# Group statistics with a PSUM operand and half a batch earlier, and GpSimd adding seven of eight key tiles

## The chip, the cores and the metric

One Trainium2 chip, one of its cores. The metric is the device time of one execution in microseconds (us), the median of several runs. The engines are TensorE (PE), VectorE (DVE), ScalarE (ACT), GpSimd (POOL) and SyncE (SP, which only starts DMAs here). [...] SBUF is the large on-chip memory.

## What is computed

The input x has 8 batches of 256 channels by 32 x 32 positions, float32. Four blocks follow each other:

```python
x = L0(x)   # attention over 1024 positions in 32 latent channels, then over 128 concepts, both added to x
x = L1(x)   # 10 class maps per position, normalised, a gate per class from their mean, added to x
x = L2(x)   # group norm (32 groups of 8 channels), qkv, attention with 8 heads of 32 channels
            #   over 1024 positions, projection, added to x
x = L3(x)   # group norm, qkv, attention between the 8 heads at each position, projection, added to x
```

L2 is the longest. Its core, for each batch and head, is

```python
weight = softmax(einsum('bct,bcs->bts', q * scale, k * scale))
a = einsum('bts,bcs->bct', weight, v)
```

and before it, as before L3, stands the group norm: the mean and variance of 8 channels by 1024 positions, by which x is shifted and scaled.

## The kernel before, in words

All of a batch's 256 channels lie on 128 partitions in two parts (t = 0, 1). The attention of L0 and L2 runs in **windows**. A window handles four heads at once, so L0 has two windows (four batches each) and L2 has sixteen, two for each batch: `par` 0 with the first four heads and `par` 1 with the others. A window has 16 steps, 8 key tiles (`mt`) of 128 keys for each of two halves of 512 queries. In a step TensorE makes the scores of one key tile for four heads (`scores`, L604, four matmuls for each head), ScalarE takes their exponentials into `PR` (L995), and TensorE multiplies the exponentials of the step before with v into the bank `AV` (`values`, L630). `PR` holds four steps.

The softmax needs a maximum for each query ahead of the scores. Maxima of the coming half are made as further jobs: one `max` job is four matmuls (L592) and four row maxima on VectorE (L1249). Scores, maxima and all small products share a ring of seven PSUM banks; each engine walks the same written order of uses (`Ring`), and TensorE waits when the bank's last reader isn't done.

**The sums of the softmax.** The sum over keys of the exponentials is made for each half. GpSimd adds the exponentials of tiles 0 to 5 (`POOL_TILES`) into `ACC`: five additions for each of two head pairs, ten instructions at L1158. Then TensorE, in the job `sums` (L646), in the first step of the next half, sums over partitions with a matrix of ones: tiles 6 and 7 straight from `PR` (L652) and `ACC` (L657), for four heads each. GpSimd's first addition of a half waits until the sums of the half before have read `ACC` (`half_done`). ScalarE copies the sums and `AV` away (`keep_half`, L962), a DMA folds the sums into `R16`, VectorE takes the reciprocal in step 2 (`invert`, L1266), a DMA returns it in step 3 (`return_inverse`), and in step 5 TensorE spreads it and VectorE multiplies (`spread`, `normalise`).

**The order of the jobs** is written by `window_jobs` (L110): for each step a list, in which every engine finds its part. Eight `max` jobs lie in the first seven steps of a half, two of them in the first. Query and key products (`qk`), v products (`v`) of the coming window and the output products of the batch before (`post`) are spread over the steps.

**The group statistics** of the next batch stand in the second half of the `par` 0 window (in the last batch: of the last window, for L3). `statistics` (L1278) reads the batch from `XIN` in SBUF with four `bn_stats` and two `bn_aggr` in step 8. `group_sums(0)` (L682) in step 10 averages the channel means over a group on TensorE; `group_stats(0)` (L1289) copies the mean (`MG`), subtracts (`DEV`, L1294), squares (L1295) and adds the variance (`S2`, L1296). Step 12 has the second group sum; then GpSimd makes the scale and shift (`norm_factors`, L1121) and writes the normalised batch `XN` (L1138). SyncE loads the next batch into `XIN` once that is done (`sp_iteration`, L469).

L3 has no windows: for each of 64 token tiles GpSimd multiplies 7 of 8 heads' weights with v (L1184), VectorE the eighth (L1589), VectorE sums (L1600), and TensorE projects. `statistics` and `group_stats` of coming batches stand in VectorE's order there too (L1626, L1636).

Of the kernel before, what the change touches and what calls it, by code (L numbers as in the profile page):

```python
# [25 lines left out]
D = 32  # L26
# [6 lines left out]
POOL_TILES = (0, 1, 2, 3, 4, 5)  # L33
POOL_SUMS = len(POOL_TILES) - 1
INVERT_AT = 2
RETURN_AT = 3
SPREAD_AT = 5
# [72 lines left out]
def window_jobs(post=False, nxt=True, gn=False, trail=True, single=False):  # L110
# [45 lines left out]
def after_jobs():  # L156
# [3 lines left out]
    jobs[2].append(("spread", -1))  # L160
# [21 lines left out]
def program(nc, x, w_l0, w_o, concepts, concepts_t, gammas, conv_w, conv_wt, conv_b, lin1_t, lin2_t,  # L182
# [8 lines left out]
    with ctx:  # L191
# [208 lines left out]
        def iteration(i, window):  # L400
# [144 lines left out]
        def _(pe):  # L545
# [84 lines left out]
            def values(u, par, s):  # L630
                half, mt = s // MT, s % MT
                if mt == 0:

                    wait(pe, half_kept, 2 * (2 * u + half))
# [69 lines left out]
            def window(u, par, jobs, i):  # L704
                for s in range(STEPS):
# [3 lines left out]
                    elif ("sums",) in jobs[0]:  # L709
                        values(u - 1, 1 - par, STEPS - 1)  # L710
                    for job in jobs[s]:
# [20 lines left out]
                        elif job[0] == "gn":  # L732
                            group_sums(job[1], i + 1)
# [224 lines left out]
        def _(act):  # L958
# [3 lines left out]
            def keep_half(u, par, half):  # L962

                wait(act, half_done, 2 * u + half + 1)
                wait(act, norm_done, 2 * u + half)
                nc.scalar.activation(RC[:, :], RING[ring.place()], ACT.Copy).then_inc(half_kept, 1)
                nc.scalar.activation(OH[par][half], AV[:, :], ACT.Copy).then_inc(half_kept, 1)

                wait(act, half_kept, 2 * (2 * u + half) + 1)
# [9 lines left out]
            def window(u, par, jobs, i):  # L979
                early = par == 1 and i is None  # L980
                for s in range(STEPS):
                    for h in range(H):
# [3 lines left out]
                        if one == 0:  # L986
# [6 lines left out]
                            else:  # L993
# [4 lines left out]
                                             ).then_inc(exp_done, 1)  # L998
                    for job in jobs[s]:
                        if job[0] == "sums" and s == 0:  # L1000
                            keep_half(u - 1, 1 - par, 1)
                        elif job[0] == "sums":
                            keep_half(u, par, 0)
                        else:
                            ring.skip(places(job, i is None))
                    if s == (1 if early else RETURN_AT) and ("sums",) in jobs[0]:
# [34 lines left out]
            keep_half(1, 1, 1)  # L1041
# [46 lines left out]
            keep_half(2 * B + 1, 1, 1)  # L1088
# [29 lines left out]
        def _(pool):  # L1118
# [22 lines left out]
            def window(u, par, jobs, i):  # L1141
                for s in range(STEPS):
# [17 lines left out]
                    if jobs and ("gn", 1) in jobs[s]:  # L1160
                        if par == 0:
# [39 lines left out]
        def _(dve):  # L1201
# [76 lines left out]
            def statistics(batch):  # L1278
                wait(dve, xin_in, 16 * (batch + 1))
                src = XIN if not isinstance(batch, int) or batch <= B else xn3(batch - B)  # L1280
                for t in range(CT):
# [3 lines left out]
                link(nc.vector.bn_aggr(MV[:, 0, :], BN6[:, 0]))  # L1285
                link(nc.vector.bn_aggr(MV[:, 1, :], BN6[:, 1]))
                dve.sem_inc(gn_ready, 1)
# [426 lines left out]
```

## Time and profile before

| | us |
|---|---|
| median of 3 runs | 2064.46 (2063.97 to 2068.48) |
| the profiled execution | 2065.67 |
| its span, first to last instruction | 2063.7 |
| L0 and L1, up to the first window of L2 | 0 to 452 |
| L2, sixteen windows | 452 to 1614 |
| L3 | 1614 to 2064 |

The profile is of one execution. Its page gives the busy time of each engine and the costliest groups of instructions; the timeline gives instructions in order of time, neighbours of one kind merged ("x4" is four of them), and in square brackets the idle time of the engine before and what ended it. A matmul of float32 is two passes in the trace, so a group of four column-tiled matmuls is "x8".

### The profile page before, as it was taken

Reading aid. Unit: us, or ns where it says so; the run is one execution under the profiler, and the core shown is the slowest. Engines: PE = TensorE matmul, PEld = TensorE weight load, DVE = VectorE, ACT = ScalarE, POOL = GpSimd, SP = SyncE. Lnnn points to the kernel's source line nnn. Section 1 sums busy time; section 2 is a strip of 40 time slices with the busy share of each in tenths; the row PEclk is TensorE's granted clock in tenths of the full one; section 3 lists DMA queues with packets and bytes.
Section 4 is the critical chain, followed back from the end, with each engine's and each line's share of the span. In section 5 each row is a group of like instructions: output and inputs, shape, how many; then the busy total and the mean of one; then the engine's idle time right before and its main releaser. Section 6 shows DMA issues by size and latency. Waiting matters only on the chain.

```text
span 2063.7 us, 37560 instructions
## 1 busy us (share of the span) xinstructions
PE 1820.6 (88%) x15416; PEld 811.3 (39%) x15416; DVE 1485.6 (72%) x2203; ACT 786.5 (38%) x1546; POOL 1189.5 (58%) x509
## 2 busy tenths in 40 slices
PE   5987876879999999999999999999999868888884
PEld 2332322334444433433443443434443444554541
DVE  5666657787776777777777777787776148888875
ACT  0441220014454554553544544544545323333320
POOL 0471210016586675756756666567676238888896
PEclk8898888879999999999999999999999989999996
DMA  5000011030000101001001001001001121222121
GB/s 175 1 2 0 1 48 73 0 123 27 22 2 5 59 1 43 22 2 62 2 2 63 2 2 63 2 1 62 2 2 42 42 68 28 87 74 84 48 70 43
DMA packets 48160, 75.10 MB, mean 36 GB/s; under 512 B 30532, under 2 KB 30838, under 8 KB 47990
## 3 DMA queue, kind: packets, MB, share of 16 engines
q1 hardware_dynamic: 38486, 72.11, 9.9%
q8 instruction: 122, 2.00, 0.4%
q10 hardware_dynamic: 9504, 0.59, 0.3%
q14 instruction: 48, 0.39, 0.1%
HBM read 44.83 MB, written 25.17 MB: 34 GB/s over the span
## 4 chain that ended last, share of the span: by engine, by line
PE 72%; DVE 18%; issue 3%; ACT 3%; DMA 2%; POOL 1%; POOLq 0%; SPq 0%; DVEq 0%; ACTq 0%
PE AV L641 13%; PE S L615 6%; DVE MX L1249 4%; PE S L592 3%; PE RB L861 3%; PE S L678 3%; PE RB L615 3%; PE S L627 2%; PE AV L874 2%; PE S L652 2%; PE S L619 2%; DVE ENC L1600 2%; PE S L750 2%; PE RB L910 2%; DVE BN L1283 2%
## 5 line engine op out<-in xcount | busy, mean ns | idle before, releaser
L1158 POOL TENSOR_TENSOR ACC<-ACC,PR 128x1024 f32<-128x1024 f32 x288 | 671.9, 2370 | 98.4 <-ACT PR L995 98.3
L1249 DVE TENSOR_REDUCE MX<-S 128x1 f32<-128x512 f32 x644 | 410.0, 683 | 150.0 <-PE RB L592 70.8
L995 ACT ACTIVATE PR<-S 128x512 f32<-128x512 f32 x678 | 363.6, 604 | 385.8 <-PE S L627 230.7
L1158 POOL TENSOR_TENSOR ACC<-PR 128x1024 f32<-128x1024 f32 x72 | 168.9, 2368 | 554.3 <-ACT PR L995 554.3
L641 PE MATMUL AV<-PR,VT 128*32 128x512 f32 x2304 | 317.2, 623 | 2.5 <-ACT PR L995 2.3
L1249 DVE TENSOR_REDUCE MX<-RB 128x1 f32<-128x512 f32 x345 | 224.4, 683 | 76.4 <-PE S L592 62.2
L995 ACT ACTIVATE PR<-RB 128x512 f32<-128x512 f32 x312 | 175.0, 604 | 208.4 <-PE S L627 118.8
L615 PE MATMUL S<-HI 32*128 32x512 f32 x678 | 202.1, 496 | 19.9 <-DVE MX L1249 13.8
L1184 POOL TENSOR_TENSOR PR<-WO,WRK 128x1792 f32<-128x1792 f32 x32 | 155.7, 4878 | 32.9 <-DVE ENC L1600 14.9
L1184 POOL TENSOR_TENSOR PR<-WO,VT 128x1792 f32<-128x1792 f32 x32 | 154.8, 4851 | 23.7 <-DVE ENC L1600 13.8
L592 PE MATMUL S<-HI 32*128 32x512 f32 x644 | 159.8, 510 | 6.0 <-ACT PR L995 3.3
L1600 DVE TENSOR_REDUCE ENC<-PR 128x256 f32<-128x2048 f32 x64 | 146.0, 2280 | 15.1 <-issue 7.0
L619 PE MATMUL S<-LO,HI 32*128 32x512 f32 x678 | 148.0, 441 | 0.0
L1249 DVE TENSOR_REDUCE MX<-SUM 128x1 f32<-128x512 f32 x163 | 111.4, 683 | 38.1 <-PE S L592 37.7
L861 PE MATMUL RB<-X 128*32 128x256 f32 x1792 | 116.9, 403 | 21.1 <-ACT WRK L1057 11.3
L995 ACT ACTIVATE PR<-SUM 128x512 f32<-128x512 f32 x162 | 97.6, 603 | 99.5 <-PE S L627 90.6
L615 PEld LDWEIGHTS S<-HI 32*128 32x128 f32 x678 | 82.0, 185 | 134.9 <-issue 44.7
L627 PE MATMUL S<-NMR,ONER 32*128 32x512 f32 x678 | 134.5, 401 | 0.0
L623 PE MATMUL S<-HI,LO 32*128 32x512 f32 x678 | 134.0, 400 | 0.0
L592 PEld LDWEIGHTS S<-HI 32*128 32x128 f32 x644 | 60.7, 188 | 155.5 <-issue 46.0
L615 PE MATMUL RB<-HI 32*128 32x512 f32 x312 | 111.3, 490 | 8.9 <-DVE MX L1249 6.9
L592 PE MATMUL RB<-HI 32*128 32x512 f32 x345 | 110.7, 511 | 0.4
(314 smaller groups left out, 3477.7 us busy)
## 6 DMA issues: line engine op xcount, KB each, us to landing
X<-out_y SPq DMA_DIRECT2D x24, 1024.0 KB, 5.0
out_y<-X SPq DMA_DIRECT2D x16, 1024.0 KB, 4.9
X<-in_x SPq DMA_DIRECT2D x8, 1024.0 KB, 8.6
OHU<-out_y SPq DMA_DIRECT2D x8, 512.0 KB, 4.4
X<-out_y SPq DMA_DIRECT2D x8, 512.0 KB, 4.1
out_y<-X SPq DMA_DIRECT2D x8, 512.0 KB, 3.1
out_y<-OHU SPq DMA_DIRECT2D x8, 512.0 KB, 3.1
WO<-WO SPq DMA_DIRECT2D x128, 16.0 KB, 1.8
```

The lines of the kernel that those rows point to most:

```text
L592: mm(bank(), HI[par][D * h:D * h + D, 0, first:first + P], HI[par][D * h:D * h + D, 1, HALF * keys:HALF * keys + HALF], start=True, stop=T ...
L615: mm(dst[h], HI[par][row, 1, keys], HI[par][row, 0, cols], start=True, stop=False, skip_group_check=True)
L619: mm(dst[h], HI[par][row, 1, keys], LO[par][row, 0, cols], start=False, stop=False, skip_group_check=True)
L623: mm(dst[h], LO[par][row, 1, keys], HI[par][row, 0, cols], start=False, stop=False, skip_group_check=True)
L627: mm(dst[h], ONER[row, :], NMR[row, half, :], start=False, stop=True, skip_group_check=True).then_inc(st_full, 1)
L641: last = mm(AV[D * h:D * h + D, :], VT[par][:, mt, D * h:D * h + D], exps(s, h // 2)[:, HALF * (h % 2):HALF * (h % 2) + HALF], start=(mt = ...
L861: last = mm(dst[D * j:D * j + D, QUARTER * (h % 2):QUARTER * (h % 2) + QUARTER], W3[:, t, C * which + D * h:C * which + D * h + D], xn3(b) ...
L995: nc.scalar.activation(exps(s, pair)[:, HALF * one:HALF * one + HALF], RING[ring.place()], ACT.Exp, scale=1.0 if i is None else float(D) * ...
L1158: nc.gpsimd.tensor_tensor(ACC[:, pair, :], so_far, exps(s, pair), ALU.add).then_inc(pool_used, 1)
L1184: nc.gpsimd.tensor_tensor(PV[n % 2].rearrange("p (h d g) -> p h d g", h=NHEAD, d=D)[:, heads], PTK[:, st, heads, j, :].unsqueeze(2).broadc ...
L1249: nc.vector.tensor_reduce(out=MX[:, h, t, keys:keys + 1], in_=bank(), op=ALU.max, axis=AX.X).then_inc(ring_free, 1)
L1600: nc.vector.tensor_reduce(out=O3[n % 2], in_=PV[n % 2].rearrange("p (c g) -> p c g", g=NHEAD), op=ALU.add, axis=AX.X).then_inc(o_ready3, 1)
```

## The change

Three things are altered.

GpSimd adds tiles 0 to 6, twelve instructions for each half. `sums` reads only tile 7 from `PR`, and it moves from the first step of the next half to the second, between its two `max` jobs; the first step then has one `max` job. The reciprocal, its return and the spread move a step later. ScalarE's `keep_half` is split: `AV` is copied in the first step, ahead of the new half's first value product, and the sums in the second.

`group_stats(0)` works in PSUM: the difference is made once into SBUF and once into PSUM, the square has one operand in PSUM and writes PSUM, and the variance is added to it from there; the bank is freed at the end of the chain. It has one more instruction.

The statistics are split into their two parts and moved: for the batch after next in the second half of the `par` 1 window, steps 11 and 12, with the first group sum in step 13 (the first batch makes its successor's in its own `par` 0 window, steps 8 to 10). Only the second group sum and the normalisation stay in the `par` 0 window, step 12; for L3's first batch they are now in the last `par` 0 window too.

```diff
-POOL_TILES = (0, 1, 2, 3, 4, 5)
+POOL_TILES = (0, 1, 2, 3, 4, 5, 6)
-INVERT_AT = 2
-RETURN_AT = 3
-SPREAD_AT = 5
+SUM_AT = 1
+INVERT_AT = 3
+RETURN_AT = 4
+SPREAD_AT = 6
...
             for n, tile in enumerate(maxima(1 - half)):
-                jobs[first + max(n - 1, 0)].append(tile)
+                jobs[first + (n if n <= SUM_AT else n - 1)].append(tile)
...
         if half == 1 or trail:
-            jobs[first].insert(1, ("sums",))
+            jobs[first + SUM_AT].insert(1, ("sums",))
...
+    if ahead:
+        first = MT + 3 if ahead == 2 else MT
+        jobs[first].append(("stats", 0, ahead))
+        jobs[first + 1].append(("stats", 1, ahead))
+        jobs[first + 2].append(("gn", 0, ahead))
     if gn:
-        jobs[MT].append(("stats",))
-        jobs[MT + 2].append(("gn", 0))
-        jobs[MT + 4].append(("gn", 1))
+        jobs[MT + 4].append(("gn", 1, 1))
...
-            window(u, 0, window_jobs(post=not first, gn=not last, trail=not first), i)
+            window(u, 0, window_jobs(post=not first, gn=True, ahead=int(first), trail=not first), i)
-            window(u + 1, 1, window_jobs(nxt=not last, gn=last), i)
+            window(u + 1, 1, window_jobs(nxt=not last, ahead=0 if last else 2), i)
...
             def sums(n):
                 kept.add(2)
-                dst = fill(half_kept, kept, 1)
-                for mt in (MT - 2, MT - 1):
-                    for h in range(H):
-                        mm(dst[D * h:D * h + D, :], ONES[:, 0:D],
-                           exps(mt, h // 2)[:, HALF * (h % 2):HALF * (h % 2) + HALF],
-                           start=(mt == MT - 2), stop=False)
+                dst = fill(half_kept, kept, 0)
+                for h in range(H):
+                    mm(dst[D * h:D * h + D, :], ONES[:, 0:D],
+                       exps(MT - 1, h // 2)[:, HALF * (h % 2):HALF * (h % 2) + HALF],
+                       start=True, stop=False)
                 wait(pe, pool_used, 2 * POOL_SUMS * (n + 1))
...
-            def keep_half(u, par, half):
-                wait(act, half_done, 2 * u + half + 1)
+            def keep_values(u, par, half):
+                wait(act, av_done, STEPS * u + MT * (half + 1))
                 wait(act, norm_done, 2 * u + half)
+                nc.scalar.activation(OH[par][half], AV[:, :], ACT.Copy).then_inc(half_kept, 1)
+            def keep_sums(n):
+                wait(act, half_done, n + 1)
+                wait(act, norm_done, n)
                 nc.scalar.activation(RC[:, :], RING[ring.place()], ACT.Copy).then_inc(half_kept, 1)
-                nc.scalar.activation(OH[par][half], AV[:, :], ACT.Copy).then_inc(half_kept, 1)
...
                 if k == 0:
-                    nc.vector.tensor_copy(MG[:, :], src[:, 0:CT]).then_inc(ring_free, 1)
+                    mean, dev, square = src[:, 0:CT], src[:, CT:2 * CT], src[:, 2 * CT:3 * CT]
+                    nc.vector.tensor_copy(MG[:, :], mean)
+                    nc.vector.tensor_tensor(DEV[:, :], mean, MV[:, :, 0], ALU.subtract)
+                    link(nc.vector.tensor_tensor(dev, mean, MV[:, :, 0], ALU.subtract))
+                    link(nc.vector.tensor_tensor(square, dev, DEV[:, :], ALU.mult))
+                    nc.vector.tensor_tensor(S2[:, :], square, MV[:, :, 1], ALU.add).then_inc(ring_free, 1)
                     own()
-                    link(nc.vector.tensor_tensor(DEV[:, :], MV[:, :, 0], MG[:, :], ALU.subtract))
-                    link(nc.vector.tensor_tensor(S2[:, :], DEV[:, :], DEV[:, :], ALU.mult))
-                    link(nc.vector.tensor_tensor(S2[:, :], S2[:, :], MV[:, :, 1], ALU.add))
```

`statistics` gets the parts as an argument, GpSimd's `norm_apply` follows the moved job, and in L0's second window the spread of the first half moves from step 2 to step 3.

## Rows read from the trace of the kernel before

**Rows 1.** The page, busy time of each engine and share of the span
```profile
PE 1820.6 (88%) x15416; PEld 811.3 (39%) x15416; DVE 1485.6 (72%) x2203; ACT 786.5 (38%) x1546; POOL 1189.5 (58%) x509
```

**Rows 2.** Timeline of TensorE (start, us, engine, line, operation), first value product of eight windows
```profile
452.69 1.08 PE L641 MATMUL AV<-PR,VT 128*32 128x512 f32 x4
...
531.66 0.64 PE L641 MATMUL AV<-PR,VT 128*32 128x512 f32 x4
...
599.11 1.07 PE L641 MATMUL AV<-PR,VT 128*32 128x512 f32 x8
...
676.07 0.64 PE L641 MATMUL AV<-PR,VT 128*32 128x512 f32 x4
...
743.56 0.64 PE L641 MATMUL AV<-PR,VT 128*32 128x512 f32 x4
...
1417.57 0.64 PE L641 MATMUL AV<-PR,VT 128*32 128x512 f32 x4
...
1485.07 0.64 PE L641 MATMUL AV<-PR,VT 128*32 128x512 f32 x4
...
1557.55 1.04 PE L641 MATMUL AV<-PR,VT 128*32 128x512 f32 x5
```

**Rows 3.** Timeline of TensorE, the step that ends a half and the next
```profile
852.59 1.06 PE L641 MATMUL AV<-PR,VT 128*32 128x512 f32 x8
...
854.02 1.92 PE L652 MATMUL RB<-PR,ONES 128*32 128x512 f32 x16
855.77 1.04 PE L657 MATMUL RB<-ACC,ONES 128*32 128x512 f32 x8
...
859.13 1.06 PE L641 MATMUL AV<-PR,VT 128*32 128x512 f32 x8
...
862.52 1.06 PE L641 MATMUL AV<-PR,VT 128*32 128x512 f32 x8
```

**Rows 4.** Timeline of VectorE, the row maxima of one step
```profile
860.66 2.48 DVE L1249 TENSOR_REDUCE MX<-S 128x1 f32<-128x512 f32 x4 [0.90 <-PE S L592]
```

**Rows 5.** Timeline of GpSimd, the adds of one half
```profile
860.18 4.70 POOL L1158 TENSOR_TENSOR ACC<-PR 128x1024 f32<-128x1024 f32 x2 [11.94 <-ACT PR L995]
864.84 18.68 POOL L1158 TENSOR_TENSOR ACC<-ACC,PR 128x1024 f32<-128x1024 f32 x8
```

**Rows 6.** The adds by line: duration in ns min/median/max, first and last start
```profile
L1158 POOL TENSOR_TENSOR ACC<-ACC,PR x288: 2334/2369/2408, 70.8 to 1610.4; 128x1024 f32<-128x1024 f32 x144
```

**Rows 7.** Timeline of VectorE, group statistics in two windows
```profile
648.10 0.16 DVE L1294 TENSOR_TENSOR DEV<-MV,MG 128x2 f32<-128x2 f32 x1
...
780.37 2.47 DVE L1283 BATCH_NORM_STATS2 BN<-X 128x6 f32<-128x512 f32 x4
...
791.21 1.07 DVE L1294 TENSOR_TENSOR DEV<-MV,MG 128x2 f32<-128x2 f32 x1
...
794.63 2.27 DVE L1296 TENSOR_TENSOR S<-S,MV 128x2 f32<-128x2 f32 x1
```

**Rows 8.** The copy of v by line: duration in ns min/median/max
```profile
L1236 DVE TENSOR_TENSOR VT<-S,X x35: 412/415/426, 394.0 to 1530.5; 128x256 f32<-128x256 f32 x35
```

**Rows 9.** Timeline of L3, VectorE's DEV and GpSimd's products in two batches
```profile
1730.85 4.45 DVE L1294 TENSOR_TENSOR DEV<-MV,MG 128x2 f32<-128x2 f32 x1
...
1738.39 4.75 POOL L1184 TENSOR_TENSOR PR<-WO,VT 128x1792 f32<-128x1792 f32 x1 [3.11 <-DVE ENC L1600]
...
1965.32 14.58 POOL L1184 TENSOR_TENSOR PR<-WO,WRK 128x1792 f32<-128x1792 f32 x3
```

**Rows 10.** Timeline of TensorE and GpSimd, end of the last window
```profile
1597.51 0.51 PE L686 MATMUL RB<-S,CST 128*128 128x2 f32 x2 [2.87 <-DVEq L1297]
...
1608.12 4.71 POOL L1158 TENSOR_TENSOR ACC<-ACC,PR 128x1024 f32<-128x1024 f32 x2
...
1613.07 1.04 PE L657 MATMUL SUM<-ACC,ONES 128*32 128x512 f32 x8
```

**Rows 11.** One stretch of the windows view: busy time and count of each engine, granted clock
```profile
1597.60:1604.30 6.70, 6.31 (x27) 2.77 (x28) 0.34 (x2) 4.13 (x8) 6.70 (x4) 0.50 0.02 4
```

More of the change, by code:

```diff
@@ L107, in maxima, with window_jobs @@
     return [("max", half, t, keys) for t in range(TILES_HALF) for keys in range(2)]
-def window_jobs(post=False, nxt=True, gn=False, trail=True, single=False):
+def window_jobs(post=False, nxt=True, gn=False, ahead=0, trail=True, single=False):
     jobs = [[] for _ in range(STEPS)]
@@ L632, in values @@
                 if mt == 0:
-                    wait(pe, half_kept, 2 * (2 * u + half))
+                    wait(pe, half_kept, 2 * (2 * u + half) - 1)
                 if half == 0 and (u < 2 and mt == 0 or u > 1 and mt % 2 == 0):
@@ L708, in window @@
                         values(u, par, s - 1)
-                    elif ("sums",) in jobs[0]:
+                    elif ("sums",) in jobs[SUM_AT]:
                         values(u - 1, 1 - par, STEPS - 1)
@@ L960, in _ @@
             ring = Ring()
-            def keep_half(u, par, half):
-                wait(act, half_done, 2 * u + half + 1)
+            def keep_values(u, par, half):
+                wait(act, av_done, STEPS * u + MT * (half + 1))
                 wait(act, norm_done, 2 * u + half)
+                nc.scalar.activation(OH[par][half], AV[:, :], ACT.Copy).then_inc(half_kept, 1)
+            def keep_sums(n):
+                wait(act, half_done, n + 1)
+                wait(act, norm_done, n)
                 nc.scalar.activation(RC[:, :], RING[ring.place()], ACT.Copy).then_inc(half_kept, 1)
-                nc.scalar.activation(OH[par][half], AV[:, :], ACT.Copy).then_inc(half_kept, 1)
-                wait(act, half_kept, 2 * (2 * u + half) + 1)
+                wait(act, half_kept, 2 * n + 2)
                 act.dma_start(R16[:, :],
@@ L998, in window @@
                                              ).then_inc(exp_done, 1)
+                    if s == 0 and ("sums",) in jobs[SUM_AT]:
+                        keep_values(u - 1, 1 - par, 1)
+                    if s == MT:
+                        keep_values(u, par, 0)
                     for job in jobs[s]:
[L1000 to L1003, printed above, removed]
+                        if job[0] == "sums":
+                            keep_sums(2 * u - 1 + s // MT)
                         else:
                             ring.skip(places(job, i is None))
-                    if s == (1 if early else RETURN_AT) and ("sums",) in jobs[0]:
+                    if s == (2 if early else RETURN_AT) and ("sums",) in jobs[SUM_AT]:
                         return_inverse(2 * u - 1)
@@ L1159, in window @@
                                                     ALU.add).then_inc(pool_used, 1)
-                    if jobs and ("gn", 1) in jobs[s]:
-                        if par == 0:
+                    if jobs and ("gn", 1, 1) in jobs[s]:
+                        if i < B - 1:
                             norm_apply(i + 1)
@@ L1276, in normalise, with statistics @@
                 dve.sem_inc(norm_done, 1)
-            def statistics(batch):
+            def statistics(batch, parts=(0, 1)):
                 wait(dve, xin_in, 16 * (batch + 1))
-                src = XIN if not isinstance(batch, int) or batch <= B else xn3(batch - B)
-                for t in range(CT):
+                src = XIN if batch <= B else xn3(batch - B)
+                for t in parts:
                     for half in range(2):
@@ L1284, in statistics @@
                 link(last)
-                link(nc.vector.bn_aggr(MV[:, 0, :], BN6[:, 0]))
-                link(nc.vector.bn_aggr(MV[:, 1, :], BN6[:, 1]))
-                dve.sem_inc(gn_ready, 1)
+                for t in parts:
+                    last = nc.vector.bn_aggr(MV[:, t, :], BN6[:, t])
+                link(last)
+                if 1 in parts:
+                    dve.sem_inc(gn_ready, 1)
             def group_stats(k, batch):
@@ L1337, in window @@
                         elif job[0] == "stats":
-                            statistics(i + 1)
+                            statistics(i + job[2], (job[1],))
                         elif job[0] == "gn":
-                            group_stats(job[1], i + 1)
+                            group_stats(job[1], i + job[2])
                         elif job[0] == "post":
@@ L1344, in window @@
                             after(0, job)
-                    if s == (1 if early else INVERT_AT) and ("sums",) in jobs[0]:
+                    if s == (2 if early else INVERT_AT) and ("sums",) in jobs[SUM_AT]:
                         invert(2 * u - 1)
```

10 lines of the change are left out of this document (6 added, 4 removed).

## The prediction

> **What bounds the kernel now.** I read first the page's busy times: TensorE 88% of the span, GpSimd 58%, VectorE 72% [rows 1]. Then I asked the timeline for the value products that open each window of the middle stage, since their starts give every window's length [rows 2]. The sixteen windows are numbered W1 to W16 here, two for each of eight batches. A W with an even number lasts 67.45 us (531.66 to 599.11; 676.07 to 743.56 and 1417.57 to 1485.07 agree). The odd ones hold the group statistics: W1 78.97, W3 76.96, and W5, W7, W9, W11, W13 together 674.01 less four even ones (270.0), so 404.0, or 80.8 each. W15, without statistics, takes 72.48. So statistics cost about 8 us a batch.
>
> Inside a window a plain step is a loop between TensorE and VectorE: 3.39 us from one value product to the next [rows 3], in which VectorE's four row maxima take 2.48 and it then sits idle 0.90 for TensorE [rows 4]. TensorE sets the pace by a little; VectorE has 0.9 us to give, and work above that lengthens the step. The step that ends a half takes 6.54 (852.59 to 859.13) since it also holds a second tile of maxima and the sums. GpSimd begins its ten adds 1.05 us after the first value product of a half and needs 4.66 + 18.68 = 23.3 us [rows 5], against a mean half of 33.7 us in an even window and 40 in an odd one: it is no bound now.
>
> **Part 1, the sums.** Four groups of four column-tiled matmuls from PR start 0.44 us apart (854.02 to 855.77 for four groups); two groups are removed, 0.87 us for each half. They lie in TensorE's order between two fills, so the time is on the path. Thirty of the 36 sums are in the steady windows, and two more in the first attention window, whose pace is alike: 32 x 0.87 = 27.7. The other four are in the stage with the small latent products, where I take nothing (bound 0 to 1.7 gained, or a few us lost, because the fold of the inverse comes a step later there), and at the end (part 4). Some gain could come on top where a query or key product now follows the sums and covers the wait for the copied bank, up to 0.4 x 15 = 6; I leave it out.
>
> What the sums wait for: GpSimd now makes twelve adds, 12 x 2.335 = 28.0 (none of 288 took over 2.408 [rows 6]). It may start when the sums of the half before have read ACC. With T the last value product of a half, the sums end at T + 3.4 (one step) + 1.4 + 4 x 0.44 + 0.2 = T + 6.8, and GpSimd ends at T + 34.9. The next sums want it at T + H + 5.7, H the length of the half. H must stay above 29.2. A mean half of an even window, less 0.87, is 32.9, and its second half, which has fewer products, is the shorter one, so 2 to 4 us are to spare; the half with the normalisation puts some 3 us more on GpSimd (an estimate; the rows above don't show them) but is longer by as much and more. The score buffers come free with the adds: the fifth step's exponentials wait for tile 0 and 1, ready at T + 11.6 when they are wanted near T + 20; the tile 6 buffer is free at T + 34.9 and wanted after T + H + 8. The copy of AV that the next half's first product now waits for stands on ScalarE behind one step's four exponentials; a whole step, 3.4 us, lies between T and that product, and the copy of the sums, with its DMA, follows a step later on the same queue, behind the next four. The query and key products behind the sums lose nothing. Nothing is late next.
>
> **Part 2, the group statistics in the middle stage.** The row to see is the pair [rows 7]: DEV takes 0.16 us at 648.10, where GpSimd happened to be idle, and at 791.21, with GpSimd adding, the three operations on two SBUF operands take 794.63 + 2.27 - 791.21 = 5.69. Each is held to the end of a GpSimd add. The maxima and the inverse's reciprocal queue behind them, and TensorE finds no free bank. The change gives each of these a PSUM operand. An addition of PSUM and SBUF operands, VT, never took over 0.426 in 35 runs beside GpSimd [rows 8], so I take 0.16 to 0.2 for each of the five new ones. The Trainium skill (SBUF - State Buffer, "Who interferes with whom") says that a VectorE instruction with two SBUF inputs contends with a GpSimd instruction that reads SBUF and one with a single SBUF input does not; the trace agrees, 5.69 against 0.16. A rule that speaks against the edit is in VectorE: DVE Perf Modes, "Rules for kernel authors": copy a matmul output to SBUF first if many operations follow. By it the chain loses tenths of a us a batch, and the sum some us in all; no row here prices so small an operand in PSUM against one in SBUF.
>
> Removed: against a statistics-free odd window of 72.48 + 0.4 (two v parts sit in other steps), W3 loses 4.1, the five loaded ones 404.0 - 5 x 72.88 = 39.6, and W1 10: at least 78.97 - 72.88 = 6.1, and it lacks four output products of four passes each, 0.87 by the spacing above. Sum 53.7. Added: the last group sum stays in the odd window, one small product and one small operation, 0 to 0.9, I take 0.4, seven times (W3 to W15), and W15 gets the other v placing, 0.4: 3.2. W1 keeps its own: one burst over the idle time 0.8 (the other lies in the step with two v parts, where TensorE is the longer), the group operations 0.4 + 0.4, so 1.6. In seven even windows VectorE gets two bursts, each half of the old 2.47 of bn_stats plus one aggregate and its waits, 1.65, of which 0.9 falls in idle time: 2 x 0.8. The group operations take 5 x 0.2 + 0.24 = 1.2, over the idle time 0.4. Together 2.0 a window, 14 in all. The bounds are 0 (if idle time elsewhere takes it up) and 4 (the whole 4.5 of work, less one idle gap). Net 53.7 - 3.2 - 1.6 - 14 = 34.9.
> The load of XIN that the earlier statistics need is released by the normalisation of the batch before, in the odd window, 45 us ahead: hidden.
>
> **Part 3, the last stage.** Five times VectorE is held 4.4 us by DEV (1730.85), and GpSimd's next product then starts 3.11 late; in the batch without statistics the same three products follow each other without a gap, 14.58 [rows 9]. GpSimd and VectorE are both near full there. I take GpSimd's 3.1 less 0.3 for the longer chain, 5 x 2.8 = 14; the ends are 0 and 5 x 4.3 = 21.
>
> **Part 4, the last window.** W16 has no maxima in its second half: its steps are near 2.2 us, and GpSimd becomes the bound. Before, its last add ends at 1608.12 + 4.71 = 1612.83 and the sums follow at 1613.07 [rows 10]. In the new one, counted from T = 1557.55 - 6.55 = 1551.0: first adds done at T + 34.9, sums 1.1, second adds 28.0, done at T + 64.1, sums at 1615.2: 2.1 later, though the 2.87 wait and the slow clock after it [rows 10, 11] are gone. TensorE stands about 11 us before that, longer than the 2.87 after which the clock row shows 0.50 for 6.7 us, so the front products start at half clock: 2 more (0 to 3.4). Cost 4.1.
>
> **The sum.** 27.7 + 34.9 + 14 - 4.1 = 72.5. The profiled execution took 2065.67 (span 2063.7), 1.2 above the median of 2064.46; from the median, 1992.
>
> **The rivals.** (a) The last stage doesn't gain: the gap goes to GpSimd's next wait, for the DMA of the weights behind it. For it: VectorE makes those weights and each step there hangs on the other engine. Against: the batch without the stall [rows 9]. Then 2006. (b) The moved statistics cost three times as much, because VectorE-bound steps leave TensorE waits that also drop its clock, as the 2.87 wait did [rows 10, 11]: 7 x 4 more, 2020. Against: each wait there would be 0.8. (c) The change doesn't do what it says: the hold needs only one SBUF operand. Then the 5.69, less the 1.2 counted above, comes to the even windows and the hold stays in the last stage: 7 x 4.5 and 14 more, so 2037. VT's 0.426 speaks against it. (d) Slower: GpSimd sets every half. Its cycle is 12a + 1.35, a one add's time, against a mean half of 36.3 before; it costs more than before from a = 2.92, through the sums' wait for ACC, behind which every later product queues. At a = 3.0 it is 32 x 1.05 = 34 above, less 14: 2085. The adds have never taken over 2.408, and the change puts no reader of two SBUF operands beside them. [...]
>
> **How the numbers follow.** The forecast 0.70, (a) 0.12, (b) 0.09, (c) 0.05, (d) 0.02, the rest 0.02 for something near no change. The forecast's own bounds: the even windows 0 to 4 (14 either way), last stage up to 7 more, first windows 3 either way, sums up to 6 more: 1976 to 2010. The range takes (a) in and reaches to (b): 1974 to 2021. A measurement of this kernel tells apart about 0.2%, 4 us. Faster 0.95, same 0.02, slower 0.03.
>
> **What would show it.** DEV and S2 at 0.16 to 0.2 us everywhere; even windows near 67.5 - 1.7 + 2.0 = 67.8, odd ones near 71.5 with no step of 9; L657's first matmul without a wait for ACC except in W16, with a wait near 11 us at the end; in the last stage no gap of 3.1 before the product behind the group statistics. Wrong would be: adds over 2.5 us, half-clock stretches in even windows, a wait of the sums for GpSimd in the steady windows.

## The result, and the profile after

The changed kernel takes 1994.41 us (median of 4 runs, 1990.84 to 1996.76) against 2065.7 of the kernel before beside it: a ratio of 0.9652, 95% interval 0.9631 to 0.9674. The forecast was 1992. The profiled execution is the fastest of the four: 1990.84, its span 1989.0.

The page, busy times:

```profile
PE 1756.6 (88%) x15128; PEld 798.8 (40%) x15128; DVE 1430.6 (72%) x2219; ACT 787.3 (40%) x1546; POOL 1358.9 (68%) x581
```

Against [rows 1] TensorE has 288 matmuls and 64.0 us less, GpSimd 72 adds and 169 us more, and VectorE 55 us less although it has 16 instructions more. What it lost is time in which it was held: summed over the trace, L1294 to L1296 of the kernel before take 66.4, their four successors (L1308 to L1311) 10.2.

The timeline of TensorE, first value products of W3 to W6 (start, us), to set beside [rows 2]:

```profile
584.26 0.64 PE L645 MATMUL AV<-PR,VT 128*32 128x512 f32 x4
...
655.12 0.64 PE L645 MATMUL AV<-PR,VT 128*32 128x512 f32 x4
...
724.72 0.64 PE L645 MATMUL AV<-PR,VT 128*32 128x512 f32 x4
...
795.62 0.64 PE L645 MATMUL AV<-PR,VT 128*32 128x512 f32 x4
```

W3 lasts 70.86, W4 69.60, W5 70.90. The odd windows came down from some 80.8 to 70.9; the even ones went up from 67.5 to 69.3 (484.8 for the seven, W2 to W14).

VectorE's group statistics by line (ns min/median/max, first and last start), and GpSimd's adds:

```profile
L1308 DVE TENSOR_TENSOR DEV<-RB,MV x10: 148/150/164, 352.5 to 1851.3; 128x2 f32<-128x2 f32 x10
...
L1309 DVE TENSOR_TENSOR RB<-RB,MV x10: 156/158/172, 352.6 to 1851.4; 128x2 f32<-128x2 f32 x10
...
L1170 POOL TENSOR_TENSOR ACC<-ACC,PR x360: 2332/2375/4389, 68.6 to 1555.2; 128x1024 f32<-128x1024 f32 x180
```

PSUM is the memory that the matmuls write to; here VectorE and ScalarE read it, and the new chain also has VectorE write there. With an operand in PSUM no instruction of the chain is held any more, in any of its 16 places (the four successors take 0.148 to 0.172); in [rows 7] the three old ones took 5.69 together. An even window of the changed kernel, TensorE and then VectorE:

```profile
707.00 1.07 PE L645 MATMUL AV<-PR,VT 128*32 128x512 f32 x8
...
709.25 0.35 PE L689 MATMUL SUM<-MV,CST 128*128 128x2 f32 x2 [0.75 <-DVEq L1301]
...
712.53 1.69 PE L645 MATMUL AV<-PR,VT 128*32 128x512 f32 x8
```

```profile
707.53 1.27 DVE L1295 BATCH_NORM_STATS2 BN<-X 128x6 f32<-128x512 f32 x2
...
711.66 0.15 DVE L1308 TENSOR_TENSOR DEV<-SUM,MV 128x2 f32<-128x2 f32 x1
```

The group sum stands one step behind the second burst and waits 0.75 for its aggregate (L1301). Behind the wait the clock is halved, as the windows view shows (length, busy times, granted clock after POOL's count):

```profile
710.40:713.80 3.40, 3.30 (x22) 1.37 (x21) 1.81 (x8) 1.58 (x4) 3.40 (x2) 0.50 0.00 0
```

0.50 is the 1.2 GHz level; the step from 707.00 to the next value product takes 5.53, where it takes 3.40 without any statistics (e3 below) and 4.07 with them but without the wait (e6). Five of the seven even windows have such a stretch. W2 and W6 have the same wait and no half clock behind it, and W6 takes 68.10, no more than a window of e6: what costs here is the half clock, not the wait itself. The end of the last window, GpSimd and then TensorE:

```profile
1529.65 4.72 POOL L1170 TENSOR_TENSOR ACC<-PR 128x1024 f32<-128x1024 f32 x2 [1.30 <-PE S L660]
1534.33 23.22 POOL L1170 TENSOR_TENSOR ACC<-ACC,PR 128x1024 f32<-128x1024 f32 x10
```

```profile
1545.87 1.04 PE L655 MATMUL SUM<-PR,ONES 128*32 128x512 f32 x8
...
1557.61 1.94 PE L660 MATMUL SUM<-ACC,ONES 128*32 128x512 f32 x8 [10.70 <-POOL ACC L1170]
```

The adds end at 1557.55 and the sums start at 1557.61: GpSimd sets this end. In [rows 10] it didn't quite: the adds had ended 0.24 before the sums began, and TensorE, itself late by the held chain, came to them without a wait. Now TensorE waits 10.70, its granted clock is 0.50 from 1550.1 to 1560.3, and its eight sums take 1.94 where [rows 10] has 1.04.

**Where the 74.7 us of the span went**, by starts of the first and last instruction of each stretch. The move of the sums puts one `max` job less ahead of a window's first value product (the step before it takes 3.40 instead of 6.55), so that mark stands 3.15 earlier; this is taken out of the first and third row.

| | before | after | difference | forecast |
|---|---|---|---|---|
| up to W1 | 452.7 | 444.1 | -8.6 + 3.15 = -5.4 | -1.7 |
| W1 to W15 | 1104.9 | 1052.7 | -52.2 | -61.0 |
| W16 to L3's first product on GpSimd | 121.2 | 129.4 | +8.2 - 3.15 = +5.0 | +4.1 |
| L3, first to last product | 362.9 | 343.1 | -19.8 | -14 |
| behind it | 22.1 | 19.7 | -2.4 | 0 |

The total was met within 2 us, but two of its terms were 9 and 6 us off in opposite directions. The experiments are about those.

### The profile page after: what moved, and what is told of

It reads as the page before. It is cut to its first block, busy times and chain, and to the rows that moved or that the text cites. A ratio compares the mean times of both kernels' runs of the same rounds, so it can differ in the third digit from the quotient of the medians.

```text
span 1989.0 us, 37180 instructions
## 1 busy us (share of the span) xinstructions
PE 1756.6 (88%) x15128; PEld 798.8 (40%) x15128; DVE 1430.6 (72%) x2219; ACT 787.3 (40%) x1546; POOL 1358.9 (68%) x581
## 4 chain that ended last, share of the span: by engine, by line
PE 77%; DVE 13%; issue 4%; ACT 2%; DMA 2%; POOL 1%; SPq 0%; POOLq 0%; DVEq 0%; ACTq 0%
PE AV L645 13%; DVE MX L1261 6%; PE S L619 6%; PE RB L864 6%; PE S L681 3%; PE S L596 3%; PE AV L877 3%; PE RB L619 3%; PE RB L913 2%; PE S L631 2%; PE S L753 2%; PE S L623 2%; PE RB L596 2%; PE RB L681 2%; PE S L671 2%
## 5 line engine op out<-in xcount | busy, mean ns | idle before, releaser
L1170 POOL TENSOR_TENSOR ACC<-ACC,PR 128x1024 f32<-128x1024 f32 x360 | 841.9, 2382 | 69.2 <-ACT PR L1003 69.2
L1261 DVE TENSOR_REDUCE MX<-RB 128x1 f32<-128x512 f32 x335 | 218.1, 683 | 75.5 <-PE S L596 60.6
L1003 ACT ACTIVATE PR<-RB 128x512 f32<-128x512 f32 x321 | 179.9, 604 | 191.2 <-PE SUM L631 81.9
L619 PE MATMUL S<-HI 32*128 32x512 f32 x673 | 193.8, 492 | 6.2 <-DVE NMR L1274 3.1
L596 PE MATMUL S<-HI 32*128 32x512 f32 x648 | 158.2, 509 | 6.0 <-ACT PR L1003 3.3
L623 PE MATMUL S<-LO,HI 32*128 32x512 f32 x673 | 141.5, 429 | 0.0
L1261 DVE TENSOR_REDUCE MX<-SUM 128x1 f32<-128x512 f32 x169 | 115.4, 683 | 35.6 <-PE S L596 35.0
L631 PE MATMUL S<-NMR,ONER 32*128 32x512 f32 x673 | 130.3, 396 | 0.0
L627 PE MATMUL S<-HI,LO 32*128 32x512 f32 x673 | 130.0, 395 | 0.0
L619 PEld LDWEIGHTS S<-HI 32*128 32x128 f32 x673 | 78.1, 183 | 109.5 <-issue 38.6
L864 PE MATMUL RB<-X 128*32 128x256 f32 x1792 | 111.8, 390 | 10.1 <-ACT X L1068 4.1
L596 PEld LDWEIGHTS S<-HI 32*128 32x128 f32 x648 | 60.2, 187 | 145.4 <-DVE MX L1261 51.5
```

What stands on the lines that cost most here:

```text
L596: mm(bank(), HI[par][D * h:D * h + D, 0, first:first + P], HI[par][D * h:D * h + D, 1, HALF * keys:HALF * keys + HALF], start=True, stop=T ...
L619: mm(dst[h], HI[par][row, 1, keys], HI[par][row, 0, cols], start=True, stop=False, skip_group_check=True)
L623: mm(dst[h], HI[par][row, 1, keys], LO[par][row, 0, cols], start=False, stop=False, skip_group_check=True)
L627: mm(dst[h], LO[par][row, 1, keys], HI[par][row, 0, cols], start=False, stop=False, skip_group_check=True)
L631: mm(dst[h], ONER[row, :], NMR[row, half, :], start=False, stop=True, skip_group_check=True).then_inc(st_full, 1)
L864: last = mm(dst[D * j:D * j + D, QUARTER * (h % 2):QUARTER * (h % 2) + QUARTER], W3[:, t, C * which + D * h:C * which + D * h + D], xn3(b) ...
```

## The experiments

Each time is the median, each ratio stands against the kernel before on the same chip. "The windows" below are W1 to W15 in the trace, which is of one execution; "the odd ones" are eight, "the even ones" seven. Between executions, and between kernels whose code is the same up to a place, single stretches differ by several us, as is said where it matters.

| kernel | us | ratio, 95% interval |
|---|---|---|
| e1_chain | 2010.12 | 0.9721 (0.9696 to 0.9746) |
| e2_sums | 2068.16 | 1.0005 (0.9988 to 1.0022) |
| e3_sums_chain | 2001.61 | 0.9679 (0.9654 to 0.9704) |
| the change | 1994.41 | 0.9652 (0.9631 to 0.9674) |
| e4_after_oldchain | 2046.97 | 0.9897 (0.9868 to 0.9925) |
| e5_last_half | 1982.54 | 0.9586 (0.9570 to 0.9601) |
| e6_group_sum_later | 1989.36 | 0.9617 (0.9596 to 0.9638) |
| e7_eight_tiles | 2059.53 | 0.9964 (0.9951 to 0.9978) |
| e8_both | 1975.42 | 0.9562 (0.9536 to 0.9587) |
| e9_six_tiles | 2014.66 | 0.9755 (0.9729 to 0.9781) |
| e10_quarters | 1970.89 | 0.9541 (0.9517 to 0.9566) |
| e11_old_place_last | 1981.00 | 0.9580 (0.9562 to 0.9598) |

**The parts alone.** e1 is the kernel before with the new chain and nothing else:

```diff
-                    nc.vector.tensor_copy(MG[:, :], src[:, 0:CT]).then_inc(ring_free, 1)
+                    mean, dev, square = src[:, 0:CT], src[:, CT:2 * CT], src[:, 2 * CT:3 * CT]
+                    nc.vector.tensor_copy(MG[:, :], mean)
+                    nc.vector.tensor_tensor(DEV[:, :], mean, MV[:, :, 0], ALU.subtract)
...
+                    nc.vector.tensor_tensor(S2[:, :], square, MV[:, :, 1], ALU.add).then_inc(ring_free, 1)
```

> The kernel before with one part of the change: the group statistics' chain has a PSUM operand in each step; sums, tiles and places stay. Theory A (the held VectorE operations are what the statistics cost): the steps of 9 us in the odd windows fall to about 4.8, the last window loses its 8 us of wait and slow clock, the last stage gains 14 to 20. Together about 57 us less than before: 2009. Theory B (most of the statistics' cost is the burst in one step and its place, which the move cures): the loaded windows keep 3 or more of their 8 us and the gain is 35 or less: 2030 or above.

Measured 2010.12. In its trace the chain takes 0.15 to 0.17 an instruction between other work of GpSimd:

```profile
777.81 0.15 DVE L1294 TENSOR_TENSOR DEV<-S,MV 128x2 f32<-128x2 f32 x1
777.88 0.16 DVE L1295 TENSOR_TENSOR S<-S,MV 128x2 f32<-128x2 f32 x1
778.07 0.17 DVE L1296 TENSOR_TENSOR S<-S,DEV 128x2 f32<-128x2 f32 x1
```

This one edit is four fifths of the whole gain: 36 us in the windows (all of it in the odd ones, 632.4 to 596.1) and 22 in L3. The total came as expected, but not the last window's part, 8 us: from W16 to L3's first product it takes 124.4 instead of 121.2. TensorE is no longer late there and waits for GpSimd:

```profile
1573.27 1.94 PE L657 MATMUL SUM<-ACC,ONES 128*32 128x512 f32 x8 [6.61 <-POOL ACC L1158]
```

So the last half was GpSimd's already with ten adds, hidden behind the held chain.

e2 is the kernel before with seven tiles and the sums a step later, the chain untouched:

```diff
-POOL_TILES = (0, 1, 2, 3, 4, 5)
+POOL_TILES = (0, 1, 2, 3, 4, 5, 6)
...
+SUM_AT = 1
```

> The kernel before with the other part: GpSimd adds seven tiles and the sums stand a step later; chain and place of the statistics stay. By the forecast's terms: 27.7 gained for the matmul groups, 4.1 and the 1.4 of the scale and shift lost in the last window where GpSimd is the bound, 4 lost in W3, where GpSimd is no longer idle when the chain comes: 2065.7 - 27.7 + 9.5 = 2047.5. Rival: more adds hold VectorE longer at each collision, or GpSimd delays the sums in steady windows: less than 10 gained.

Measured 2068.16 (ten runs, 2061.99 to 2074.96), no gain at all and 21 above the expectation. The forecast's term of 27.7 for the sums doesn't stand alone. The steady even windows do go from 67.49 to 66.20. The odd ones W5 to W13 stay where they were, 80.81 and 80.85. In all the windows gain 2 us (even ones 6.8 less, odd ones 4.8 more). The chain in eight odd windows of e2, by line, is first, and the same lines of the kernel before follow:

```profile
L1303 DVE TENSOR_TENSOR DEV<-MV,MG x8: 1064/1073/2230, 493.7 to 1582.2; 128x2 f32<-128x2 f32 x8
...
L1304 DVE TENSOR_TENSOR S<-DEV x8: 2268/2274/2302, 494.8 to 1584.4; 128x2 f32<-128x2 f32 x8
```

```profile
L1294 DVE TENSOR_TENSOR DEV<-MV,MG x8: 164/1074/2166, 498.2 to 1590.5; 128x2 f32<-128x2 f32 x8
...
L1295 DVE TENSOR_TENSOR S<-DEV x8: 160/2274/2294, 499.3 to 1592.7; 128x2 f32<-128x2 f32 x8
```

In the kernel before, W3's chain met GpSimd idle (the 0.16 of [rows 7]) and escaped. With twelve adds it is held in every batch, so W3 takes 80.48 instead of 76.95. The steps around the chain also got longer: from the eleventh to the thirteenth value product it is 15.92 instead of 15.20, the mean of W5 to W13. That isn't the reciprocal that moved into them, for without the held chain the same steps take 9.11 with or without the move (e3, e1). Most of it is the clock. W5 and then W7, first in the kernel before, then in e2:

```profile
791.13:805.81 14.68, 11.60 (x67) 4.53 (x66) 12.72 (x17) 4.01 (x8) 10.37 (x5) 0.88 0.01 1
938.88:954.82 15.94, 12.95 (x67) 5.26 (x66) 12.96 (x17) 4.01 (x8) 10.52 (x6) 0.79 0.01 1
```

```profile
790.87:805.60 14.73, 11.59 (x68) 4.38 (x67) 13.10 (x17) 4.01 (x8) 10.64 (x5) 0.88 0.01 1
937.40:953.78 16.38, 13.25 (x67) 5.13 (x66) 13.32 (x17) 4.02 (x8) 10.85 (x6) 0.79 0.01 2
```

In the kernel before two of the five windows are of the second kind (0.79), in e2 four. L3 shows 370.0 instead of 362.9 with the same instructions in it, which is no more than the spread of that stretch (below).

e3 has both edits, and the statistics in their old place:

> Both parts without the third: the statistics stay where they were in the kernel before. Theory A: the move itself is worth little, since what it takes from the odd windows (a burst of 2.9 us of VectorE of which only 1 to 2 shows) it gives to the even ones (3.5 us measured after): within 5 us of the changed kernel, 1990 to 2000. Theory B: the move is worth the burst and more: 2004 to 2010.

Measured 2001.61, between the two. Against e1 the windows gain 17.2 (odd 596.1 to 585.9, even 472.4 to 465.5). The stretch from W16 to L3 loses 9.2 - 3.15 = 6.1, which leaves 11 in these two; by the medians the two kernels are 8.5 apart. What the changed kernel has beyond e3 is the move of the statistics: odd windows -18.1, even ones +19.3, so nothing in the windows.

e4 is the changed kernel with the old chain back:

```diff
-                    nc.vector.tensor_tensor(DEV[:, :], mean, MV[:, :, 0], ALU.subtract)
...
+                    link(nc.vector.tensor_tensor(DEV[:, :], MV[:, :, 0], MG[:, :], ALU.subtract))
+                    link(nc.vector.tensor_tensor(S2[:, :], DEV[:, :], DEV[:, :], ALU.mult))
```

> The changed kernel with the old chain on two SBUF operands put back, in the new place. Theory A: each of eight collisions costs 4.5 to 5.7 us in the windows, and five of 3 to 4 us in the last stage: 36 to 45 and 15 to 20 more than 1994.4, so about 2050. Theory B (the place matters more than the operands): 2010 to 2020.

Measured 2046.97: the PSUM operand is worth 52.6 in the new place too. It also shows what rival (c), a hold that remains, would have cost: the even windows rise to 519.0 (34.2 above the changed kernel; the rival's price was 31.5) and L3 to 369.3. One line of its trace shows how far the hold goes, VectorE and then GpSimd:

```profile
1297.00 9.42 DVE L1308 TENSOR_TENSOR DEV<-MV,MG 128x2 f32<-128x2 f32 x1
```

```profile
1283.18 23.22 POOL L1170 TENSOR_TENSOR ACC<-ACC,PR 128x1024 f32<-128x1024 f32 x10
```

The subtraction ends at 1306.42 and the tenth add at 1306.40. At 2.32 an add, four adds ended in between (at 1297.2, 1299.5, 1301.8 and 1304.1) without letting the small instruction in; it ran when GpSimd had no further one. That window lasts 78.78, the other six even ones 73.1 to 74.5.

**The last window.** In e5 the last half alone is shared out differently: GpSimd adds tiles 0 to 3, and TensorE, which waits there anyway, reads tiles 4 to 7.

```diff
-                wait(pe, pool_used, 2 * POOL_SUMS * (n + 1))
+                added = LAST_SUMS if n == LAST_HALF else POOL_SUMS
...
+                wait(pe, pool_used, 2 * (POOL_SUMS * n + added))
...
-                    if mt in POOL_TILES[1:]:
+                    if mt in POOL_TILES[1:] and (2 * u + half < LAST_HALF or mt <= LAST_SUMS):
```

> The changed kernel, but in the very last half GpSimd adds only tiles 0 to 3 and TensorE reads tiles 4 to 7 from PR (three more groups, 1.3 us). If the 11.6 us for which TensorE waited for ACC there is GpSimd's bound, the last sums come about 10 us earlier and the front products of the last stage run at the full clock (2 to 3 us more): 1994.4 - 11 = 1983. Rival: the wait only moves to the exponentials or to the fold of the sums behind it: 1990 or above.

Measured 1982.54, as expected. TensorE:

```profile
1553.06 3.62 PE L659 MATMUL SUM<-PR,ONES 128*32 128x512 f32 x32
1556.49 1.04 PE L664 MATMUL SUM<-ACC,ONES 128*32 128x512 f32 x8
```

No wait stands between, and the sums take 1.04, at full clock. From the last value product to the end of the sums it is 5.4 instead of 14.6. So 12 us of the changed kernel lie in that one half.

e11 is e3 with the same edit, and so differs from e5 only in where the statistics stand:

> The third kernel (sums and chain changed, statistics in their old place) with the fifth's edit: in the last half GpSimd adds only tiles 0 to 3. It asks where the 7 us by which the move was worth it come from, when the steady windows of both kernels add up to the same. Theory A: from the last window, out of which the move takes the statistics; then with the last half relieved the old place is still behind the fifth kernel's 1982.5 by what the group sums' waits cost there, 3 to 7: 1986 to 1990. Theory B (spread between executions): 1981 to 1984.

Measured 1981.00 against 1982.54, so not the 1986 to 1990 that the first theory gave: once the last half is relieved, the move of the statistics in this form brings nothing. Of the 7.2 that it had brought the changed kernel over e3, 4.2 lie from W16 to L3's first product (133.7 in e3, 129.4 in the changed kernel; 120.0 in e11 and 118.5 in e5, with the last half relieved). The other 3 have no place: they are of the size by which L3 differs between executions. e3's timeline of GpSimd shows one reason for the 4.2, part of the normalisation's work in the middle of the adds that set the end:

```profile
1552.69 0.69 POOL L1138 TENSOR_TENSOR RSTD<-VE,MHALF 128x2 f32<-128x2 f32 x1
...
1554.28 9.24 POOL L1167 TENSOR_TENSOR ACC<-ACC,PR 128x1024 f32<-128x1024 f32 x4
```

**The moved statistics.** In e6 the first group sum stands a step later, so that its aggregate is long done:

```diff
-        jobs[first + 2].append(("gn", 0, ahead))
+        jobs[first + (3 if ahead == 2 else 2)].append(("gn", 0, ahead))
```

> The changed kernel with the first group sum one step later in the even windows (step 14 in place of 13). Theory A: the 1.5 us by which an even window is dearer than forecast come from the group sum's wait of 0.75 us for the second burst, behind which the scores queue, and from the half clock that follows in five of seven windows: about 1.5 x 7 = 10 less, 1984. Rival: the cost is VectorE's full load in steps 11 to 13, wherever the group sum stands: within 3 us of 1994.4.

Measured 1989.36, 5 us less, between the two. The even windows fall from 69.26 to 68.35 each (478.5 for seven), all seven now alike within 0.02. The 0.75 wait and the half clock behind it so cost 0.9 a window, and the statistics without it 68.35 - 66.20 = 2.15 (66.20 is a steady even window of e3, which has none).

e8 has the edits of e5 and e6, e10 spreads the four bursts of e8 over four steps, one each:

```diff
-        jobs[first].append(("stats", 0, ahead))
-        jobs[first + 1].append(("stats", 1, ahead))
+        for part in range(4):
+            at = first + part - 1 if ahead == 2 else first + part // 2
+            jobs[at].append(("stats", part, ahead))
```

> The fifth and the sixth kernel's edits together. If both theories hold and their places are independent: 1994.4 - 11 - 10 = 1973. If only the end gains: 1983.

> The eighth kernel with the even windows' statistics cut in four bursts of 0.6 to 0.9 us in steps 10 to 13 in place of two of 1.5 in steps 11 and 12. Theory A: a VectorE burst costs only what goes beyond the 0.9 us that it is idle in a step; then four quarters are nearly free and the seven even windows fall from 68.35 to about 66.8: 10 less than 1975.4, 1965. Rival (every us of VectorE there shows): no change, 1973 to 1978.

Measured 1975.42, as expected within 2.5, and 1970.89, the fastest kernel here; the latter lies between its theory (1965) and its rival (1973 to 1978). Against e11, with the same last half and the statistics in their old place, the moved statistics are worth 5.6 in e8 and 10.1 in e10: the move pays once its group sum stands a step later. VectorE in an even window of e10:

```profile
706.68 2.48 DVE L1266 TENSOR_REDUCE MX<-S 128x1 f32<-128x512 f32 x4 [0.41 <-PE S L599]
709.08 0.68 DVE L1300 BATCH_NORM_STATS2 BN<-X 128x6 f32<-128x512 f32 x1
```

One burst of 0.68 fits into the idle time of a step and leaves 0.41 of it: the three steps with one burst and no more take 3.46 or 3.47 instead of 3.40. The even windows W4 to W14 take 67.33, not the 66.8 expected; the statistics cost 1.1 a window instead of 2.15, and 0.65 of that is the step with the fourth burst, which is 4.0 long without it and 4.65 with it.

**How many tiles.** e9 is the changed kernel with six tiles again, the sums still a step later; e7 gives GpSimd all eight.

```diff
-POOL_TILES = (0, 1, 2, 3, 4, 5, 6)
+POOL_TILES = (0, 1, 2, 3, 4, 5)
```

> The changed kernel with GpSimd adding six tiles again, TensorE reading tiles 6 and 7 from PR, and everything else (sums a step later, chain, moved statistics) as changed. Theory A: of the sums' part the tile is worth its matmul group in each half, 32 x 0.44 = 14, less what the seventh tile costs in the last window, 4.7 and some slow clock: 1994.4 + 14 - 6 = 2002. Rival (GpSimd's seventh tile costs as much as it saves, through holds of VectorE and the last window): within 3 of 1994.4 or below it.

Measured 2014.66: the seventh tile is worth 20.3. The expectation has a slip: a tile is two of the groups that start 0.44 apart, so 0.87 a half and not 0.44, 26 us in the windows. By the traces it is 18.1 there (odd 575.2 to 567.8, even 495.5 to 484.8): 0.6 a half, or 0.77 where the steady windows alone are taken (72.36 to 70.86, 70.98 to 69.42 as the mean of W4 to W14), because W1 is 3.1 longer. W1 in e9, then in the changed kernel:

```profile
453.27:521.95 68.68, 67.38 (x530) 29.82 (x528) 52.44 (x94) 34.62 (x68) 50.39 (x26) 1.00 0.30 112
```

```profile
444.13:515.92 71.79, 70.18 (x523) 30.34 (x522) 52.45 (x94) 34.63 (x68) 58.52 (x30) 0.93 0.29 108
```

The granted clock is 1.00 in one and 0.93 in the other. In e5, e6 and e8, whose code up to the end of W1 is the changed kernel's, W1 takes 74.74, 74.72 and 71.73 at 0.89, 0.89 and 0.93. So the 3.1 are the clock's, and no price of the seventh tile is read from W1.

> The changed kernel with all eight tiles added by GpSimd, so that its cycle is 14 x 2.345 + 1.35 = 34.2 us against halves of 34.5 to 35.5. The forecast's account of the cycle: another 0.44 us a half less on TensorE, at most 14 gained, but now the sums wait for GpSimd in the even windows' halves and in the half with the normalisation (34.2 + 3.3), and the end is 4.7 us later: between 1985 and 2000, with waits of the sums for ACC in many windows. Rival (GpSimd has room): 1985 or less and no waits except at the end.

Measured 2059.53, 65 above the changed kernel. The expectation was wrong by 60 us. It had GpSimd's load, the normalisation (34.2 + 3.3) and the waits of the sums in it, but put no price on the waits. GpSimd:

```profile
793.58 13.99 POOL L1166 TENSOR_TENSOR ACC<-ACC,PR 128x1024 f32<-128x1024 f32 x6 [0.66 <-ACT PR L999]
...
809.16 2.37 POOL L1146 TENSOR_SCALAR X<-X,GA,GB 128x1024 f32<-128x1024 f32 x2
811.50 13.98 POOL L1166 TENSOR_TENSOR ACC<-ACC,PR 128x1024 f32<-128x1024 f32 x6
```

Then TensorE:

```profile
820.60 1.07 PE L645 MATMUL AV<-PR,VT 128*32 128x512 f32 x8
...
825.62 1.94 PE L656 MATMUL S<-ACC,ONES 128*32 128x512 f32 x8 [3.51 <-POOL ACC L1166]
```

Fourteen adds (32.7) and the normalisation (807.53 to 811.5, 4.0) are 36.7, against a mean half of 35.4 in this window. The sums wait 3.51, run at half clock (1.94), and the even windows from W4 on take 74.2, 4.8 more than in the changed kernel. Over the whole trace the sums wait for ACC twenty times, 58.0 together, 21.6 of it from the start of W16 on. The windows are 35.7 longer than in the changed kernel, the stretch before them 13.9 and the one from W16 to L3 12.9. That is rival (d)'s mechanism, set off by the number of adds and not by their length.

## Why the prediction was right

**The chain, right.** The hold needs two SBUF operands, and one in PSUM removes it. This was read from 5.69 against 0.16 and from VT's 0.426 [rows 7, 8]; 148 to 172 ns in the changed kernel and e1's 57 us show it. The prediction's own comparison showed only the hold: its 0.16 is of two SBUF operands with GpSimd idle, and the case of one operand rested on VT. The Trainium skill (SBUF - State Buffer, "Who interferes with whom") states that a VectorE instruction with two SBUF inputs contends with a GpSimd instruction that reads SBUF, and one with a single SBUF input, outside the two-port modes, does not. The traces agree in both directions, 0.15 to 0.17 in e1 and up to 9.42 in e4. The Trainium skill's rule to copy a matmul output to SBUF first if many operations follow (VectorE: DVE Perf Modes, "Rules for kernel authors") doesn't hold for this chain: from PSUM an instruction takes 0.15 to 0.17 here, from SBUF 0.16 where it isn't held and up to 9.42 where it is.

**The statistics in L2, right in sum.** Forecast 34.9; by e1 (36.3) and the step from e3 to the changed kernel (18.1 in the odd windows, -19.3 in the even ones) 35.1. Its parts were less exact: the odd windows gained 54.4 where 48.9 net was forecast, and the even ones lost 19.3, not 14; so part of the agreement is luck. The 2.0 a window was right for the work itself (e6: 2.15). What was left out is the wait for the aggregate with the clock drop behind it. Rival (b) named this mechanism and priced it at 4 more a window; it costs 0.9. "Each wait there would be 0.8" was right (0.75), but it was taken as too short to matter to the clock, which it isn't in five windows of seven.

**The sums, mis-sized.** The term was 0.87 a half, 26.1 in the windows; it measured 17.2 (e1 to e3) and, for the tile alone, 18.1 (e9 to the changed kernel). The spacing was read from TensorE alone. From e1 to e3 the steady even windows gain 1.29 of the 1.74: the steps around the two sums give 1.6, and the steps behind them, with the spread one later, take 0.3 back. The steady odd ones gain 2.0, but W1 to W3 together lose 1.8 instead of gaining 5.2. W1's granted clock is 0.99 in e1 and 0.93 in e3, and W2's last step takes 5.58 in e3 where it is 3.40 in W4: the first windows lose to half-clock stretches what the sums give. What sets these off is open. Nor did the text see that parts can depend on each other: beside the held chain the same edit is worth nothing (e2).

**The last stage, mis-sized.** Forecast 14, bounds 0 and 21; measured 19.8, and e4 shows 369.3 against the changed kernel's 343.2. The price of a hold was capped at GpSimd's 3.11 late start [rows 9]. The stretch is 362.9 to 370.0 long in the three kernels with the old chain and 338.9 to 346.2 in ten with the new one, though each group has one code there, so single executions differ by 7; 17 to 31 is what can be said. In part the clock goes with it: 0.95 granted over the stretch where it takes 338.9 (e5), 0.93 where it takes 345.5 (e6). Rival (a) is refuted. No product of GpSimd starts late behind the group statistics any more:

```profile
1672.40 14.62 POOL L1196 TENSOR_TENSOR PR<-WO,VT 128x1792 f32<-128x1792 f32 x3
```

**The last window, right.** Forecast: second adds done at T + 64.1, a wait near 11, 4.1 us lost. Measured from T = 1493.41: 64.1, 10.70, and 5.0 lost. The 0.9 beyond it is the sums themselves at half clock. What it had not seen is that this end was GpSimd's before too, once the held chain is taken away (e1's wait of 6.61). The text charged this as the price of the change; e5 shows that one edit of that half alone takes it back, and 7 us more.

**No wait for GpSimd in steady windows, right.** L660 waits for ACC twice in the whole trace, 0.32 and 10.70, both in W16. The margin of 2 to 4 us was real and no more: e7's two further adds, 4.7 us, used it up.

**One sign of "wrong" did occur.** An add took 4.39, near 190 us, beside an instruction of VectorE's with two large SBUF operands (below); what it costs there wasn't tried. And half-clock stretches did appear in even windows. Neither moved the total out of the range, which the start (-5.4 where -1.7 was forecast; the mark at 444.1 stands at 446.6 to 448.1 in e5, e6 and e8, whose code up to there is the same, so 2 to 4 of it are spread) and L3 held up against the sums. The total of 1992 is thus partly luck: 9 us too much for the sums, 12 too little for the start, L3 and what follows it.

## What to carry to other kernels

A small instruction of VectorE's with two SBUF operands beside a busy GpSimd can take as long as the rest of GpSimd's instruction, and longer; look for such durations, give the instruction a PSUM operand, and do that before costing anything else, since the hold hides what other edits are worth. When work moves to a helper engine, count everything that engine does in its fullest half, price the wait and the half clock that follow if it doesn't fit, and share the last round out anew, where nothing is left to hide the helper behind. Small bursts belong one to a step, each within that step's idle time, and whoever needs their result a whole step behind the last of them.

## What the runs showed of the hardware

- A held VectorE instruction mostly gets in at the end of GpSimd's running one (2.27 a time in L2, 4.5 beside one product of 4.87 in L3), but once it was passed over for 9.42 us, at four ends of adds (e4). What decides that is open.
- The hold works the other way round too. VectorE's multiplication of two SBUF operands waited here for the first of two adds to end, ran, and held the second: two adds took 6.69, one of them 4.39 where 2.3 is usual. The multiplication took 3.50; the same one at 216.83, alone, took 2.29.

```profile
189.00 3.50 DVE L1404 TENSOR_TENSOR WRK<-WRK,CR 128x2048 f32<-128x2048 f32 x1
```

```profile
188.01 6.69 POOL L1170 TENSOR_TENSOR ACC<-ACC,PR 128x1024 f32<-128x1024 f32 x2 [8.48 <-ACT PR L1003]
```

- TensorE's clock fell to 0.50 for 3.4 us or more behind a wait of 0.75 (five windows of seven), and for 10.2 us at the 10.70 wait. In the other two windows the same wait was followed by no fall. Without the 0.75 wait (e6) none of the seven has a half-clock stretch, and they agree within 0.02.
